# A vision tower with routed experts on one core: centred patch weights, slot arithmetic in other operations, a new row order for the expert products, dummy products in other places, and another order of the first four routed tiles

## What is computed

```
tokens = einsum('bnd,ed->bne', patchify(x), W) + b            # 16 x 36 patches, 768 -> 256
h = concat([cls, tokens], axis=1) + pos_embedding             # 592 tokens of 256
h = layernorm(h + attn_block(h))                              # its own first step: layernorm(h)
scores = softmax(h @ gate_w.T); topk_w, topk_idx = top_k(scores, 3)
a = gelu(g) * xh * geglu_mult                                 # xh, g = halves of h @ fc1_w[e].T + fc1_b[e]
y = sum over the token's three experts e of  w_e * (a @ fc2_w[e].T + fc2_b[e])
out = layernorm(h + y + shared_expert(h))
```

## Time and profile before

| | us |
|---|---|
| median of three runs | 218.86 (218.07 to 219.18) |
| the profiled execution, its own time | 218.37 |
| its span (first to last instruction) | 216.6 |
| so around the span | 1.8 |
| PE busy | 202.2 (93%) |
| POOL, DVE, ACT busy | 120.4, 106.7, 94.4 |

### The profile page before, as it was taken

The page is one execution under the profiler, slowest core; times in us unless marked ns, Lnnn a source line. Parts: engine busy times, 40 slices in busy tenths (PEclk is TensorE's granted clock), DMA queues, the critical chain, the costliest instruction groups (busy, mean ns, idle before and its releaser), DMA issues.

```text
span 216.6 us, 4391 instructions
## 1 busy us (share of the span) xinstructions
PE 202.2 (93%) x1551; PEld 128.4 (59%) x1551; DVE 106.7 (49%) x295; ACT 94.4 (44%) x219; POOL 120.4 (56%) x148
## 2 busy tenths in 40 slices
PE   7999899989998899989999999899999999998952
PEld 4777577667886675756877763354444555445510
DVE  4076587748973444275579943523334222230044
ACT  2003543568868373553438672233323333324023
POOL 0040099649979867949998077407756652257000
PEclk9999999999999999999999999999999999999975
DMA  6999999920000299941021023319975321112692
GB/s 220 396 394 351 410 420 419 414 113 5 6 3 3 78 381 369 420 111 48 3 98 30 0 73 102 99 33 339 371 275 193 92 73 53 48 48 98 166 229 88
DMA packets 15054, 38.30 MB, mean 177 GB/s; under 512 B 2713, under 2 KB 6298, under 8 KB 15034
## 3 DMA queue, kind: packets, MB, share of 16 engines
q1 hardware_dynamic: 13018, 32.53, 41.7%
q0 software_dynamic: 2016, 5.51, 8.2%
HBM read 29.25 MB, written 4.06 MB: 154 GB/s over the span
## 4 chain that ended last, share of the span: by engine, by line
PE 81%; DVE 6%; DMA 6%; ACT 2%; issue 1%; POOL 1%; SPq 1%; POOLq 0%; DVEq 0%; ACTq 0%
PE ps L364 70%; DMA wres<-y_dram 3%; PE ps L1798 3%; PE ps L1609 2%; PE ps L1838 2%; PE ps L1622 2%; DMA embed_sb<-embed 2%; DMA y_dram<-ln_mem,dest_i 1%; PE ps L1542 1%; POOL y_dram L644 1%; DVE ln_mem L990 1%; DVE nw_i L974 1%; DVE nw L979 1%; DVE nw L980 1%; SPq L421 1%
## 5 line engine op out<-in xcount | busy, mean ns | idle before, releaser
L364 PE MATMUL ps<-wres,cT 128*64 (+1 forms) x360 | 62.9, 468 | 1.7 <-DVE cT L1363 0.6
L364 PEld LDWEIGHTS ps<-wres,cT 128*64 128x64 f32 (+1 forms) x360 | 25.5, 131 | 29.4 <-issue 22.2
L644 POOL DMA_INDIRECT y_dram<-ln_mem,dest_i x21 | 20.7, 985 | 27.3 <-ACT ln_mem L852 24.0
L407 POOL TENSOR_TENSOR wres<-wres,fac_mem 128x512 f32<-128x512 f32 x22 | 27.2, 1272 | 2.9 <-DVE ln_rs L981 2.9
L635 POOL DMA_INDIRECT embed_sb<-x_dram,gather_i x21 | 20.4, 971 | 13.5 <-DVE gather_i L1303 6.5
L1356 DVE TENSOR_TENSOR h<-ps,h 128x256 f32<-128x256 f32 x21 | 8.1, 420 | 33.0 <-PE ps L1838 24.9
L846 ACT ACTIVATE h<-ps 128x256 f32<-128x256 f32 x21 | 8.1, 384 | 30.1 <-PE ps L364 30.1
L364 PE MATMUL ps<-h,stage 128*128 128x296 f32 x64 | 18.0, 419 | 0.0
L852 ACT ACTIVATE ln_mem<-ps 128x256 f32<-128x256 f32 x21 | 8.1, 384 | 16.4 <-PE ps L364 16.4
L1363 DVE COPY cT<-ps 128x256 f32<-128x256 f32 x21 | 8.8, 423 | 10.3 <-PE ps L364 8.7
L364 PEld LDWEIGHTS ps<-h,stage 128*128 128x128 f32 x64 | 11.7, 190 | 3.7 <-issue 0.4
(11 more groups left out here) (208 smaller groups left out, 379.4 us busy)
## 6 DMA issues: line engine op xcount, KB each, us to landing
wres<-experts SPq DMA_DIRECT2D x15, 768.0 KB, 13.4
fac_mem<-experts SPq DMA_DIRECT2D x11, 256.0 KB, 8.1
embed_sb<-embed SPq DMA_DIRECT2D x6, 416.0 KB, 5.2
wres<-ut SPq DMA_DIRECT2D x3, 768.0 KB, 8.9
stage<-shared SPq DMA_DIRECT2D x2, 771.0 KB, 16.4
wres<-y_dram SPq DMA_DIRECT2D x4, 384.0 KB, 5.7
stage<-wres SPq DMA_DIRECT2D x2, 512.0 KB
f1v<-fc_v SPq DMA_DIRECT2D x1, 512.0 KB
```

Of the source, the lines that this page charges most:

```text
L364: return nc.tensor.matmul(o, w, x, start=start, stop=stop)
L407: nc.gpsimd.tensor_tensor(w1(e, c), w1(e, c), row, ALU.subtract).then_inc(less_done, 1)
L644: pool.indirect_dma_start(out=y_dram[:, :], out_offset=bass.IndirectOffsetOnAxis(ap=dest_i[:, column(i):column(i) + 1], axis=0), in_=ys[:, ...
```

## The change

In the order of the program:

1. **Embedding.** The first chunk is loaded in two pieces, weights and patches. DVE sums each row of the chunk's weights and subtracts the mean from it (`centre_chunk`), and PE waits for that instead of the load. `place_biases` adds bias, position and class token once, before the products end; PE takes the mean of these 39 columns ahead of chunk 4 (`bias_means`), and DVE adds the centred sum and the product straight into `xc`. `h0`, `mean` and `centre` are gone.
2. **Routing.** `positions` moves from unit 3 to unit 2 and `choose` with it; `groups_hot` moves to unit 3, all of `places_hot` to unit 4, `tables` to unit 5, and `slot_table` from the start of unit 7 to the start of unit 6. The table stands in bank 3. In `slots` and `choose` operations with one tensor and constants give way to operations with two tensors, and one conversion goes away.
3. **Routed tiles.** The first two tiles are transposed before `down(7)`, each of tiles 2 and 3 behind `first` of tile 0 and 1, ACT's loading of the gelu table comes behind `tile_in(0)` and `(1)`, and `a_r` has four buffers, in `fac_mem`.
4. **End.** The rows of a partition in `y_dram` lie side by side, so that a read takes 4 KB in one piece from each of 96 partitions where it took four pieces of 1 KB. Ten dummy products stand between the first products of the end instead of eight behind them, and three more ahead of each of the last four reads' products.

```diff
@@ layout
-YROWS = NT * P + KS * NSUM
+YROWS = NT * P + KS * PC * TT
+NAR = 4
-        a_r = h1_mem[:, 2 * F:4 * F].rearrange("p (a f) -> p a f", a=2)
+        a_r = fac_mem[:, 0:NAR * F].rearrange("p (a f) -> p a f", a=NAR)
+        y_sums = y_dram[NT * P:YROWS, :].rearrange("(p c) d -> p c d", p=KS)
@@ read_rows
-            eng.dma_start(yr[:, lo:hi],
-                          y_dram[NT * P + KS * lo:NT * P + KS * hi, :].rearrange("(c p) d -> p c d", p=KS)) \
-                .then_inc(ld_y[t], 16)
+            eng.dma_start(yr[:, lo:hi], y_sums[:, lo:hi]).then_inc(ld_y[t], 16)
@@ sync
-            for k in range(KP):
+            sp.dma_start(tw_sb[:, 0], embed[:, 0, 0:D]).then_inc(ld_emb[0], 16)
+            sp.dma_start(pt_sb[:, 0], embed[:, 0, D:EC]).then_inc(ld_pt, 16)
+            for k in range(1, KP):
@@ scalar
-            warm(ACT.Gelu)
...
             tile_in(0)
             tile_in(1)
+            warm(ACT.Gelu)
             for j in range(0, NT, 2):
                 for i in range(j, min(j + 2, NT)):
                     gate(i)
+                    if j == 0:
+                        tile_in(i + 2)
                 for i in range(j + 2, min(j + 4, NT)):
-                    tile_in(i)
+                    if j:
+                        tile_in(i)
@@ vector
+            def centre_chunk(k):
+                dve.wait_ge(ld_emb[k], 16)
+                nc.vector.tensor_reduce(tw_sum[:, k:k + 1], tw_sb[:, k], AX.X, ALU.add).then_inc(tw_cen, 1)
+                dve.wait_ge(tw_cen, 2 * k + 1)
+                nc.vector.scalar_tensor_tensor(tw_sb[:, k], tw_sum[:, k:k + 1].to_broadcast([P, D]), -1.0 / D,
+                                               tw_sb[:, k], ALU.mult, ALU.add).then_inc(tw_cen, 1)
...
+            def centre_biases():
+                dve.wait_ge(mean_mm, 1)
+                nc.vector.tensor_tensor(place_b[:, :, :], place_b[:, :, :],
+                                        ps[:, 6, 0:S + 2].unsqueeze(1).to_broadcast([P, DC, S + 2]),
+                                        ALU.subtract).then_inc(place_done, 1)
...
-                nc.vector.tensor_scalar(pick_i[:, 1], pick_i[:, 0], TM - 1, None, ALU.bitwise_and).then_inc(rt, 1)
+                nc.vector.tensor_tensor(within_i[:, :], pick_i[:, :], low_bits[:, :], ALU.bitwise_and).then_inc(rt, 1)
+                nc.vector.scalar_tensor_tensor(upper[:, :], pick_i[:, :], NT * TM - 0.5, tm_t[:, :],
+                                               ALU.is_ge, ALU.mult).then_inc(rt, 1)
...
             def gated(i):
                 dve.wait_ge(ge_done, i + 1)
-                if i >= 2:
-                    dve.wait_ge(at_mm, i - 1)
...
+                if i == 0:
+                    dve.wait_ge(less_done, DC * E)
+                if i >= NAR:
+                    dve.wait_ge(at_mm, i - NAR + 1)
@@ tensor
             for k in range(KP):
-                pe.wait_ge(ld_emb[k], 16)
+                if k == 0:
+                    pe.wait_ge(ld_pt, 16)
+                if k == KP - 2:
+                    bias_means()
+                pe.wait_ge(tw_cen, 2 * k + 2)
...
-                if k == 3:
-                    positions()
-                if k == 7:
+                if k == 6:
                     slot_table()
...
                 if k == 6:
-                    pe.wait_ge(rt, 9)
+                    pe.wait_ge(idx_done, 1)
+                    pe.wait_ge(tab_out, 2)
                     pe.wait_ge(xr_out, 3)
+                if k == 2:
+                    positions()
...
             shared_units(unit)
             down(6, 2, 1, 1)
-            down(7, 3, 1, 1)
...
                 lower_expert(i)
                 tile_transposed(i)
+            down(7, 3, 1, 1)
             for j in range(0, NT, 2):
 
                 for i in range(j, min(j + 2, NT)):
                     first(i)
+                    if j == 0:
+                        tile_transposed(i + 2)
+                        lower_expert(i + 2)
...
                     mm(o[:, c * P:(c + 1) * P], hs[:, c, t * P:t * P + rows], ident, False, False)
-            keep_clock(2, 8)
+                keep_clock(2, 2)
             pe.wait_ge(mix_done, TOPK * PC)
             for t in range(TT):
 
+                if t:
+                    keep_clock(2, 3)
                 pe.wait_ge(ld_y[t], 16)
```

More of the change, by code:

```diff
@@ L121 @@
 C_DST, C_DUMP = _col(TOPK * TT), _col(NT)
+C_TILE_TM = _col(NT)
 NRTE = _v
@@ L664, in _, with squares @@
         def _(act):
-            def squares(ln, n, src, made, each):
+            def squares(ln, n, src, made, ahead=0):
                 for c in range(DC):
-                    act.wait_ge(made, DC * n + c + 1 if each else n + 1)
+                    act.wait_ge(made, ahead + DC * n + c + 1)
                     nc.scalar.activation(sq[:, n, c], src[:, c], ACT.Square).then_inc(ln.sq, 1)
@@ L796, in _ @@
                 if g == 1:
[L797 removed]
+                    squares(ln2, 1, half(h1, 1), op_done)
                 if g == 11:
[L799 removed]
+                    squares(ln3, 0, half(hs, 0), mo_done)
             warm(ACT.Sqrt)
[L801 removed]
+            squares(ln3, 1, half(hs, 1), mo_done)
             std(ln3, 1)
@@ L1316, in routing @@
                     slots()
+                    choose()
                 if k == 3:
-                    choose()
+                    groups_hot()
                 if k == 4:
-                    groups_hot()
-                    places_hot(0)
+                    for q in range(TOPK):
+                        places_hot(q)
                 if k == 5:
-                    places_hot(1)
-                    places_hot(2)
+                    tables()
                 if k == 6:
                     owners()
-                    tables()
                     softmax_start()
@@ L1733, in slot_table @@
                     if q == 0:
-                        pe.wait_ge(rt, 26)
-                        pe.wait_ge(t1_done, 7)
-                    last = mm(ps[:, 4, 0:3 * NT], hot[:, q],
+                        pe.wait_ge(rt, 25)
+                    last = mm(ps[:, 3, 0:3 * NT], hot[:, q],
                               hot_val[:, q].rearrange("p v i -> p (v i)"), q == 0, q == TOPK * TT - 1)
@@ L1837, in gated_transposed @@
                 for f in range(FC):
-                    last = nc.tensor.transpose(ps[:, 2 + i % 2, f * P:(f + 1) * P], a_r[:, i % 2, f * P:(f + 1) * P], ident)
+                    last = nc.tensor.transpose(ps[:, 2 + i % 2, f * P:(f + 1) * P], a_r[:, i % NAR, f * P:(f + 1) * P], ident)
                 last.then_inc(at_mm, 1)
```

150 lines of the change are left out of this document (77 added, 73 removed).

## The result

| | before | after |
|---|---|---|
| median, us (runs) | 218.69 (4) | 215.45 (4) |
| profiled execution, us | 218.37 | 215.5 |
| its span, us | 216.6 | 213.7 |
| its mean granted clock of TensorE | 0.982 | 0.994 |

The ratio is 0.9858 (95% interval 0.9831 to 0.9885): 3.2 us faster, where 3.4 (218.86 to 215.5) had been forecast. The two profiled executions lie 2.9 us apart. The sum came out; two of its four terms did not.

What follows compares the result with a forecast made beforehand. PE was taken to bound the kernel from 4.31 us, others counting only where it waits. Embedding 1.6, routing -0.1, first tiles 1.2 and end 0.4 sum to 3.1 us saved: forecast 215.5 us, range 213.6 to 217.4.

Steps and rivals of the forecast that it cites:

- The embedding, 1.6: Embedding at the start: 2.3 us off PE, 0.5 added for bias means, 0.2 later start; 1.6 saved, bounds 0.6 and 1.8.
- a product takes 0.50: Embedding products on PE: 0.50 us each, up to 0.84 if the granted clock falls to 0.50.
- the clock as a rival: Embedding: pauses around chunk 0 drop PE's clock to 0.50, the kernel takes up to 223 us; chance 0.05.
- The lower bound of 0.6: Embedding: the least saving in us, given with 1.8 as the most.
- It is carried whole: First scores: POOL starts at 27.32, its first keys end about 36.3, PE comes at 36.5; the full 1.6 us carries on.
- The routing, 0.1 lost: Shared units: PE reaches slot_table at 120.02, hot rows ready 119.6 to 120.1; 0.1 us lost, bounds 0 and 0.6.
- The reading of 0.17 against 0.33: Slot arithmetic: with POOL busy, two-tensor operations take 0.17 us and one-tensor 0.33, so choose and slots get shorter.
- The first tiles, 1.2: First routed tiles: PE's gaps go and first(4) starts at 138.0 to 138.2; 1.2 us saved, bounds 0.7 and 1.3.
- The end, 0.4: End: spread dummies hold PE's clock through the last reads' products; 0.4 us saved, or 0.9 lost if they don't.
- The rate by the partitions: End: the 96 partitions, not the size of the piece, set the rate of the y_dram reads, 240 to 250 GB/s.
- 0 for the 4 KB: End: reading 4 KB pieces instead of 1 KB gains nothing.
- The upper bound of 413: End, rival: with 4 KB pieces the reads reach 413 GB/s, 1.6 us less, 213.9 us; chance 0.25.

Runs made afterwards that it cites:

- sets 1 and 3: Two groups of follow-up runs made on the same chip; the kernel before took 220.85 us in set 1 and 220.37 in set 3.
- four combinations: Changed kernel's reads: 4 KB into 96 partitions (unaltered), 1 KB into 96 (215.63 us), 3 KB into 128 (214.45), 1 KB into 128 (214.67).
- the third expert: Changed kernel with POOL's third expert moved behind the first keys and fourteen first dummies instead of twelve: 217.37 us, ratio 0.9906.
- the kernel with both attempts: Changed kernel with fourteen first dummies, POOL's third expert behind the first keys, and reads into 128 partitions with right sums: 217.78 us, ratio 0.9921.

## Why the prediction was right

**The embedding, 1.6.** The mechanism is as described: PE drops the means over all tokens (2.3), the bias means cost 0.36 (0.5 forecast), PE starts 0.05 later instead of 0.2. What failed for the profiled execution is "a product takes 0.50": the first ones took twice that. I had the clock as a rival, as a fall that a pause would trigger. The runs show another thing: TensorE starts at the half clock, and the full one is granted at a moment that moves between executions. In thirteen traces with twelve or fourteen dummies it stands at 4.03 to 4.87 us (seven) or 6.14 to 6.88 (six), with the embedding of before as with the new one; in the one with ten dummies at 9.02. A pause of 0.4 does not put it off; whether fewer dummies do rests on that one trace and on its medians. So this term is 0.97 in one pair of traces, and about 1.5 in the medians of the experiment that puts the old embedding back. (The lower bound of 0.6 has no working: the terms named, 2.3 - 0.5 - 0.8, give 1.0.)

**It is carried whole.** This step failed. With POOL's order unchanged and the new embedding there are nine traces. In four TensorE waits 0.52 to 0.88 us for the keys, with POOL starting at 28.55 to 28.89; in the five others POOL starts at 27.08 to 27.93 and PE does not wait. I took 27.32 from one trace as if it stood still; it is the landing of a load. In the first trace, too, no more than 0.95 could have come through: POOL started at 27.93, its second keys ended at 37.04, and the scores started at 37.14, so an earlier composing would have been waited away there. Over the nine the scores start at 36.49 to 37.88, 37.25 in the mean; with the old embedding and twelve dummies they start at 38.09 and 39.29. Whether the extra load issue of the new embedding pushes the experts' loads back was not tested; three traces with the old loads have POOL at 27.20, 27.32 and 27.51, and eight of eleven with the new ones later than that. The forecast's full 1.6 shows in two of the nine, at the end of the stage: ScalarE's first row behind it (line 709 before, then 720 and 723) stands at 42.52 and 42.47 against 44.07 before.

**The routing, 0.1 lost.** Right: no wait at `slot_table`, the gather 3.25 us earlier behind the shift. The reading of 0.17 against 0.33 was too simple. With POOL busy, operations with two inputs in SBUF took 0.17 on 15 elements in two rows (lines 1262 and 1286) and 0.48 in another (1292); on 75 elements they took 0.24 (1272) and 0.45 (1270). They can be slow as well, and `choose` and `slots` lost some 0.6 us by it, an estimate from these rows; it cost nothing, since PE reached `slot_table` just as the hot rows were ready. Which operation is hit is open.

**The first tiles, 1.2.** Right: 1.1 in the trace, and with the old order back 1.3 by the medians and 0.85 by the ratios. In eight traces ScalarE stands still ahead of the first `gate`, for 2.6 us, by a releaser that the profile doesn't know; `first(2)` then starts 0.3 later and VectorE's product is the last to come:

```profile
129.24 2.62 another core or an unknown queue
...
131.88 0.39 ACT h L856
...
132.30 0.44 DVE fac_mem L1392
...
132.97 3.65 PE ps L375 x16
```

(the kernel with fourteen dummies). PE's work on the next tiles covers most of it. What it leaves is 0.35: `first(4)` stands 100.42 to 100.45 us behind the scores in six of them, 100.09 in the first trace, so the new order is worth some 0.8 there. All eight are on the chip of sets 1 and 3, and the six other traces, three with either order, don't have it. So the new order alone doesn't bring it; the old one was not traced on that chip. Its cause is open.

**The end, 0.4.** The rate by the partitions, and 0 for the 4 KB: right, shown by four combinations and by the 1 KB layout in the changed kernel. The clock: the spread dummies hold it, 0.25 us instead of 0.4 (the prediction's own terms, 1.93 against 0.64 + 0.45 + 0.5, give 0.34, and three dummies took 0.55). The reads still ran 0.45 us ahead of before, with either layout (8.35 and 8.39); why is open. The 247 GB/s is the low end of what 96 partitions got: in the same stretch behind the first issue the two traces of the kernel before have 243 and 258, the others 262 to 291. The upper bound of 413 was wrong for this layout: it belongs to 128 partitions.

So the total was right because the embedding's 0.6 too few in the profiled pair met the end's 0.3 too many (0.25 of the clock and 0.45 of earlier reads against 0.4). That these met is luck: the differences of loads and of the clock's start from run to run are of that size. The mechanisms of the first tiles and of the end's rate are not luck. The experiments give about 1.5 for the embedding, on the chip where the whole change gives 5.1, and 0.85 to 1.3 for the first tiles, on another; the clock has 0.25 (0.67 by medians whose intervals overlap), and the layout none. Each compares across sets, so they are not shares that must add up to 3.2. The routing's part by itself, and the slot arithmetic, were not undone and stay at what the trace shows. On the second chip the change gave 5.1 us (ratio 0.9751, its interval clear of the first); the kernel before was not traced on that chip, so where it loses the rest there is open.

## What to carry to other kernels

An engine's start that comes from a landed load is a distribution, not a number: price the engine next in line by several traces, or by the largest wait that it could cause. Undo one part and compare medians before you believe one pair of traces, since one part gave 0.97 us in a pair of traces and 1.4 to 2.0 in medians. Run the kernel that you compare with in the same set. Work that is moved on an engine with slack is paid where it runs next: the third expert cost 1.5 us in another engine's chain 45 us later. Ahead of the first entry in the list of clocks, read the level from the spacing of the records and not from the column.

## What the runs showed of the hardware

- TensorE started at the half clock in all fourteen traces (dummies 0.247 us apart, 0.13 at full clock). The full level came at 4.03 to 6.88 us in thirteen and at 9.02 in the one with ten dummies; there the spacing of the embedding's records goes from 0.48 to 0.24. Ahead of that the column says 1.00 because the trace has no entry yet.
- In the kernel with both attempts the clock was at 0.50 from 85.12 to 88.53, behind 5.00 us in which PE worked 3.30. With the moved expert alone PE worked 3.29 of the same 5.00 us, and the clock stayed.
- The Trainium skill (TensorE: Matmul & The Clock Gate, What's actually happening) says that the clock gate doesn't start anew with a kernel, so that the moment of the rise varies against its first product. The starts above agree, and vary more than I had expected.
- Reads of DRAM into SBUF: 268 to 325 GB/s with 96 partitions, 328 to 386 with 128, in the stretches shown, about the same for pieces of 1 and of 3 or 4 KB.
- A VectorE operation of 0.20 us on 74 elements took 0.73 and 1.20 beside POOL's products of two tensors.
